# Q's first row block from exact codes in a PSUM bank of its own, and Q's cosine product on GpSimd

## The reference

```python
def _dequant(codes, scales):
    w = codes.astype(jnp.float32) - 8.0
    return w * jnp.repeat(scales, GS, axis=0)
...
q = hidden_states @ _dequant(q_codes, q_scales)
k = hidden_states @ _dequant(k_codes, k_scales)
v = hidden_states @ _dequant(v_codes, v_scales)
...
q = _rope(q)
k = _rope(k)
...
scores = jnp.einsum('bhqd,bhkd->bhqk', q, k) * scale + mask[None, None]
attn = jax.nn.softmax(scores, axis=-1)
out = jnp.einsum('bhqk,bhkd->bhqd', attn, v)
...
return out @ _dequant(o_codes, o_scales)
```

## Time and profile before

| | before |
|---|---|
| median of 3 runs | 1103.8 us (1103.57 to 1104.54) |
| span of the profiled execution | 1104.9 us, 18938 instructions |
| mean granted PE clock | 0.992 |
| PE busy | 96% |
| DVE busy | 85% |
| ACT busy | 63% |
| POOL busy | 62% |

### The profile page before, as it was taken

One profiled execution on the slowest core, in us unless ns is written; L12 is line 12 of the kernel. 1 busy time (PEld: TensorE's weight loads), 2 busy tenths in 40 slices (PEclk: granted clock), 3 DMA queues, 4 the chain that ended last, 5 costly groups with the idle time before them and its releaser, 6 DMA issues.

```text
span 1104.9 us, 18938 instructions
## 1 busy us (share of the span) xinstructions
PE 1056.7 (96%) x5448; PEld 513.8 (47%) x5448; DVE 934.1 (85%) x1755; ACT 690.9 (63%) x1502; POOL 689.6 (62%) x770
## 2 busy tenths in 40 slices
PE   3898999899999999999999999999999999989998
PEld 2443444444544444444444444544544544444443
DVE  7977897799888888888888889999999998888873
ACT  4455665766777777777777776666666666463320
POOL 2457546877767766776777677777878777332200
PEclk9999999999999999999999999999999999999999
DMA  9344231767678667657766765777777675432453
GB/s 350 123 135 132 67 101 44 150 149 170 142 155 160 145 147 159 159 134 154 163 148 141 159 160 130 148 155 162 151 150 171 142 128 119 108 117 53 101 103 79
DMA packets 301204, 153.65 MB, mean 139 GB/s; under 512 B 249264, under 2 KB 261808, under 8 KB 301136
## 3 DMA queue, kind: packets, MB, share of 16 engines
q1 hardware_dynamic: 293360, 139.46, 55.3%
q10 hardware_dynamic: 7776, 13.37, 4.4%
HBM read 89.07 MB, written 4.19 MB: 84 GB/s over the span
## 4 chain that ended last, share of the span: by engine, by line
PE 78%; DVE 8%; ACT 5%; POOL 3%; issue 3%; ACTq 1%; DMA 1%; SPq 1%; DVEq 0%; POOLq 0%
PE side_ps L699 10%; PE side_ps L856 9%; PE side_ps L701 9%; PE side_ps L700 9%; PE proj_ps L876 8%; PE out_ps L876 8%; PE proj_ps L1027 4%; PE score_ps L839 3%; PE score_ps L841 2%; PE score_ps L840 2%; PE proj_ps L1032 2%; PE score_ps L998 2%; PE out_ps L719 2%; PE score_ps L719 2%; PE proj_ps L699 2%
## 5 line engine op out<-in xcount | busy, mean ns | idle before, releaser
L1534 POOL TENSOR_TENSOR w_b<-prob,w_b 128x896 f16<-128x896 f32 (+2 forms) x192 | 188.9, 998 | 30.6 <-ACT w_b L1222 30.0
L699 PE MATMUL side_ps<-hT,w_a 128*128 128x512 f16 x504 | 191.1, 379 | 1.5 <-DVE rot L1895 1.5
L701 PE MATMUL side_ps<-hT,w_a 128*128 128x512 f16 x504 | 191.0, 379 | 0.0
L700 PE MATMUL side_ps<-hT,w_a 128*128 128x512 f16 x504 | 191.0, 379 | 0.0
L1990 DVE SCALAR_TENSOR_TENSOR x_acc<-proj_ps,o_now,x_acc 128x1024 f32<-128x1024 f32 x120 | 153.6, 1280 | 37.8 <-PE proj_ps L876 37.8
L1527 POOL TENSOR_SCALAR prob<-prob,row_inv 128x512 f32<-128x512 f32 (+3 forms) x256 | 170.7, 681 | 22.6 <-DVE row_inv L2063 16.9
L1195 ACT ACTIVATE prob<-score_ps,neg_max 128x512 f32<-128x512 f32 (+3 forms) x256 | 132.9, 521 | 47.4 <-DVE neg_max L1966 38.6
L1541 POOL TENSOR_TENSOR q_sb<-rot,q_sb 128x512 f16<-128x512 f32 x64 | 75.0, 1172 | 139.8 <-ACT q_sb L1187 139.8
L1990 DVE SCALAR_TENSOR_TENSOR x_acc<-out_ps,o_now,x_acc 128x1024 f32<-128x1024 f32 x120 | 152.7, 1272 | 0.0
L876 PE MATMUL proj_ps<-work,w_b 128*128 128x512 f16 x496 | 127.3, 379 | 1.9 <-DVE x_acc L1990 1.1
L876 PE MATMUL out_ps<-work,w_b 128*128 128x512 f16 x496 | 127.3, 379 | 1.3 <-DVE x_acc L1990 1.2
(11 more groups left out here) (238 smaller groups left out, 2102.5 us busy)
## 6 DMA issues: line engine op xcount, KB each, us to landing
stage_c<-in_codes_dram SPq DMA_DIRECT2D x80, 256.0 KB, 2.9
stage_o<-in_codes_dram SPq DMA_DIRECT2D x64, 256.0 KB, 3.9
stage_s<-in_scales_dram SPq DMA_DIRECT2D x64, 256.0 KB, 3.8
ctx_raw<-in_ctx_dram ACTq DMA_DIRECT2D x32, 256.0 KB, 3.2
work<-w_b SPq DMA_TRANSPOSE x261, 3.0
x_acc<-in_x_dram SPq DMA_DIRECT2D x8, 512.0 KB, 8.5
k_sb<-in_codes_dram SPq DMA_DIRECT2D x16, 256.0 KB, 6.4
v_sb<-in_scales_dram SPq DMA_DIRECT2D x16, 256.0 KB, 7.3
```

The costliest lines, as they stand in the source:

```text
L699: pe.matmul(o, stat(0), mov(0), start=first, stop=False)
L700: pe.matmul(o, stat(0), mov(1), start=False, stop=False)
L701: return pe.matmul(o, stat(1), mov(0), start=False, stop=last)
L1534: ins = pool.tensor_tensor(prob16[:, 1, to:to + w], prob[:, at:at + w], prob16[:, 0, to:to + w], ALU.subtract)
```

## The change

The first row block of Q's weights (row block 0 of 8) is no longer scaled ahead of the product. Its codes less 8 are whole numbers that float16 holds exactly, so there is no lower part: `q_exact` takes two products for it (codes by upper and by lower part of the hidden states) in place of three, into `pv_ps`, the bank of `weigh`. The scale, one for each feature and so for each partition here, is applied by ACT when it copies that bank to `rot` (`q_base`). `q_part` adds up row blocks 1 to 7 in `q_ps` as before, and DVE adds both (`q_join`) into `rot`. From there swap, cosine and sum read `rot`; the cosine product, in place, is POOL's (`q_turn`), and `sine` moves with it to the head of POOL's next slot. `q_sum` moves behind O add 3. Q's of slots 0 to 3 are made as before (`by_parts`). The scales for `q_base` ride with O's in `o_table` and `o_now`, one column more; they are loaded once (`q_scale_rows`) and scaled by DVE in the prologue. `k_scale` moves into a free part of `prob`.

```diff
+            def q_exact(g, i):
+                h = i // B
+                p = g * SLOTS + i
+                pe.wait_ge(piece_done, g * SLOTS + (2 * h + 2))
+                pe.wait_ge(ao_ready, p - 3)
+                for l in range(2):
+                    mm = pe.matmul(pv_ps, w_a[:, 0, h % RING * KB * P:(h % RING * KB + 1) * P],
+                                   hT[:, l, 0, i % B * S:(i % B + 1) * S], start=l == 0, stop=l == 1)
+                mm.then_inc(q_exact_done, 1)
...
                     else:
-                        pe.wait_ge(q_summed, p)
+                        pe.wait_ge(q_joined, p - FIRST_PIECES)
...
+                if not (known(p) and (p == 0 or p >= N_SLOTS - FIRST_PIECES + 1)):
+                    pe.wait_ge(q_based, p)
...
-                if has_ahead:
+                parts = by_parts(p + Q_AHEAD)
+                if has_ahead and parts:
+                    q_exact(*ahead)
+                elif has_ahead:
                     q_part(*ahead, range(0, 1))
...
+                if exact:
+                    act.activation(w[:, 0, col:col + exact], stage_c[:, r, 0:exact], ACT.Copy, bias=-CODE_ZERO)
+                act.activation(w[:, 0, col + exact:col + PIECE], stage_s[:, r, exact:PIECE], ACT.Copy, scale=up)\
                     .then_inc(piece_hi, 1)
...
-                swap(q_bank(p), q_swapped)
+                if by_parts(p):
+                    act.wait_ge(q_joined, p - FIRST_PIECES + 1)
+                swap(rot if by_parts(p) else q_bank(p), q_swapped)
+            def q_base(g, i):
+                p = g * SLOTS + i
+                act.wait_ge(q_exact_done, p - FIRST_PIECES + 1)
+                act.wait_ge(q_ready, p)
...
+                act.activation(rot[:, :], pv_ps, ACT.Copy, scale=o_now[:, (i // B + 1) % 2, CB:CB + 1])\
+                    .then_inc(q_based, 1)
...
                 if has_piece:
                     q_cut(p, i)
+                if has_ahead and by_parts(p + Q_AHEAD):
+                    q_base(*((g, i + Q_AHEAD) if i < SLOTS - Q_AHEAD else (g + 1, i + Q_AHEAD - SLOTS)))
...
+            def q_turn(p):
+                pool.wait_ge(q_swapped, p + 1)
+                pool.tensor_tensor(rot[:, :], rot[:, :], cos_t[:, :], ALU.mult).then_inc(q_cosed, 1)
...
                         pool.wait_ge(ctx_free, q + 1)
+                    if not (known(p) and p >= N_SLOTS - 1) and by_parts(p + 1):
+                        sine(q_swapped, p + 1, q_sined)
+                        q_turn(p + 1)
...
                     prob_rest(p, 0)
-                    if not (known(p) and p >= N_SLOTS - Q_AHEAD):
+                    if not by_parts(p + Q_AHEAD):
                         sine(q_swapped, p + Q_AHEAD, q_sined)
                     prob_rest(p, 1)
...
-                dve.tensor_tensor(rot[:, :], q_bank(p), swapped[:, :], ALU.add).then_inc(q_summed, 1)
+                dve.tensor_tensor(rot[:, :], rot[:, :] if by_parts(p) else q_bank(p), swapped[:, :], ALU.add)\
+                    .then_inc(q_summed, 1)
+            def q_join(p):
+                dve.wait_ge(q_done, p + 1)
+                dve.wait_ge(q_based, p - FIRST_PIECES + 1)
+                dve.tensor_tensor(rot[:, :], q_bank(p), rot[:, :], ALU.add).then_inc(q_joined, 1)
...
-                if has_next:
+                if has_next and not by_parts(p + 1):
                     q_sum(p + 1)
                 if not (i or known(p)):
-                    maxima(p, i, 0)
+                    dve.wait_ge(q_ready, p + 1)
                 if has_o and not (known(p) and p == O_LAG):
                     o_add(p - 1, (i - 1) % SLOTS, 3)
+                if not (i or known(p)):
+                    maxima(p, i, 0)
+                if has_next and by_parts(p + 1):
+                    q_sum(p + 1)
                 maxima(p, i, 1)
...
                 if has_o:
                     o_add(p, i, 1)
                 if known(p) and wf_early(p) is not None:
                     wf_difference(wf_early(p))
+                if has_ahead and by_parts(p + Q_AHEAD):
+                    q_join(p + Q_AHEAD)
                 if has_o:
                     o_add(p, i, 2)
...
-                if has_ahead:
+                if has_ahead and not by_parts(p + Q_AHEAD):
                     q_cos(p + Q_AHEAD)
```

## The result

| | before | changed |
|---|---|---|
| median | 1104.2 us (1103.57 to 1105.71, 4 runs) | 1222.1 us (1220.46 to 1222.34, 4 runs) |
| ratio | | 1.1058 (95% interval 1.1046 to 1.1071) |
| span of the profiled execution | 1104.9 us | 1218.7 us |
| mean granted PE clock | 0.992 | 0.982 |

What follows compares the result with a forecast made beforehand. A closed loop through DVE, ACT and POOL, not PE, was to bound the changed kernel: 34 (context) + 46 (dense-weight) + 9 (group 0) + 1 (prologue) = 90 us on 1104.9, median 1194 us, range 1160 to 1230.

Steps and rivals of the forecast that it cites:

- the loop: Closed slot-to-slot chain through DVE, ACT and POOL, without PE, longer than the old period; chance 0.78, 1194 us.
- the 1.8 us stop ahead of `q_sum`: On DVE after O add 3: the moved `q_sum` waits 1.8 us for POOL's cosine, everything queued behind it waits too.
- Context slots: Groups 1 to 4, 32 slots: loop of 13.22 us against 12.15, 1.07 more each, 34 us.
- Dense-weight slots: Slots from 40 on: loop of 14.05 us against 11.98, 2.07 more in 22 slots, 46 us.
- this collision: POOL and DVE slowing each other in the new order: bounded at 0.3 us per slot, 18 us.
- Group 0: Slots 3 to 7, of the dense-weight kind (slot 7 without POOL's weight add): about 9 us more.
- The cosine: POOL's cosine product in the loop: 1.27 us by the trace, against 1.38 us and 1200 us total by the skill's rule.
- `q_base`, counted at nothing: New PSUM eviction on ACT, 0.60 us by L1231, covered by ACT's wait for POOL; 36 us without that cover.
- Nothing of PE's 13 us is left.: 60 saved PE products of 0.22 us, 13 us at most, gain nothing since PE idles 1.5 to 2.3 us a slot.
- Had the loop been open: Rival, loop does not close: PE's saved products count for 6 to 13 us, 1091 to 1098 us; chance 0.05.
- The join counted as no gain and no loss on DVE: DVE loses the cosine product and gets `q_join` instead, both 128x512 from PSUM: nothing either way.
- PE's clock: Rival: idle time in each slot also lowers PE's clock, 50 us more, about 1244 us; chance 0.07.

Runs made afterwards that it cites:

- e5: Changed kernel with one extra small POOL product per slot (0.40 us) ahead of the sine, inside the loop: 1243.2 us, ratio 1.1244.
- e6: Changed kernel with the same extra POOL product of 0.40 us placed behind the cosine, beside the loop: 1226.0 us, ratio 1.1092.
- e1: Changed kernel with sine and cosine of Q(p+2) put back between POOL's two probability rests: 1135.0 us, ratio 1.0277.
- e2: Changed kernel with the cosine product back on DVE, sine still at the head of POOL's slot: 1155.6 us, ratio 1.0456.
- e8: Changed kernel with the weight difference and `q_join` moved ahead of O add 1 on DVE: 1157.4 us, ratio 1.0474.
- e9: Changed kernel with only the dense weights' difference moved ahead of O add 1, join left behind both: 1209.5 us, ratio 1.0950.
- e10: e7 with a third product in the exact block again (the second repeated): 1113.8 us, ratio 1.0082.
- e7: Changed kernel with the moves of e1 and e8 together: 1110.4 us, ratio 1.0046.
- e4: Changed kernel with `q_join` ahead of the weight difference on DVE in dense-weight slots: 1193.7 us, ratio 1.0806.
- e12: e7 with the join behind O add 1 again in the context slots only: 1112.8 us, ratio 1.0071.
- e3: Changed kernel with the pieces' scaling and lower part over all 512 columns again in even slots: 1227.8 us, ratio 1.1113.

## Why the prediction was right, and where it was off

The forecast was 1194 us, 90 more than before; it came out at 1222.1, 118 more, in the upper part of the range of 1160 to 1230.

**What bounds the kernel, and the loop.** The order of the links, the 1.8 us stop ahead of `q_sum` (1.69 measured) and that PE has no part held. e5 against e6 shows that time counts inside the loop and little beside it (21 against 4 us), and e1, e2 and e8 each take back what they take out of it, up to the next chain. What I had missed is that there are two loops with the join in common. It made no difference to the sum, which went by the longer; it would have made one to advice: the obvious cure (e1) leaves 30 us, by size more than half of it the long difference.

**Context slots.** The sum gave 13.22 us a slot, 34 us; 13.26 and 35.7 measured. It is not luck by terms that cancel: DVE's part from `q_sum` to the join was taken as 6.36 us and is 6.35, and no other link is off by more than 0.07.

**Dense-weight slots: the term that was mis-sized.** 14.05 us were predicted, 14.87 measured, 63.5 us in place of 46. The step taken was "777.78 to 783.80 (maxima 1 to the end of the weight difference) 6.02", with the difference at the earlier trace rows's 0.47 us. In ten of the 22 slots it takes 1.92, which is by size some 14.7 of the 17.5 us; e9, which takes it away, gets 0.43 a slot back. I had bounded this collision at 0.3 us a slot by the longest L1522 and L1764 and had looked at no instruction between them. The kernel before held it once already, in the maximum of the difference's own line, from the source view of L1913:

```profile
L1913 DVE SCALAR_TENSOR_TENSOR w_b<-w_b,wf_mean x31: 467/470/1709, 191.4 to 948.8; 128x256 f32<-128x256 f32 x31
```

That one began at 675.30, 0.45 us behind the begin of rest 0. The short slots, 14.23, are 0.18 us over the sum; 0.13 of that is `q_sum`, 0.82 us beside POOL's weight clip where the context slots have 0.69. Slots 60 and 61 are 0.70 under it, since they convert no piece.

**Group 0.** 9 us predicted, 15.3 measured. Two of its differences take 1.92 us, which is 2.9 of the 6.3 us more. The rest wasn't separated.

**The cosine.** 1.27 us by the earlier trace rows; its own row in the changed kernel, with those of `q_base` and `q_sum`:

```profile
L1591 POOL TENSOR_TENSOR rot<-rot,cos_t x60: 1254/1265/1276, 219.7 to 1044.4; 128x512 f32<-128x512 f32 x60
```

```profile
L1227 ACT ACTIVATE rot<-side_ps,o_now x60: 667/670/687, 211.6 to 1036.0; 128x512 f32<-128x512 f32 x60
```

```profile
L1953 DVE TENSOR_TENSOR rot<-rot,swapped x60: 691/693/827, 221.0 to 1045.8; 128x512 f32<-128x512 f32 x60
```

The row came closer than the rule of the Trainium skill ("GPSIMD Engine Reference", section Engine selection: about twice VectorE's time): 1.265 against 0.69 us is 1.8 times.

**`q_base`, counted at nothing.** 0.67 us, not the 0.60 of L1231; it stood under ACT's wait, as said. In context slots, where the split behind it waits for nobody, it is part of what delays ACT; the loop, which enters ACT at the swap, doesn't see it.

**"Nothing of PE's 13 us is left."** PE is idle for 13% of the changed kernel's span and its chain is not PE's; no run puts the product back there. Had the loop been open I gave 6 to 13 us for it; e10 measures 3.4.

**The join counted as no gain and no loss on DVE** was right in DVE's work (934.1 and 945.9 us busy, of which the twelve long differences alone add some 17), wrong as a way of seeing it: unlike the cosine that it replaces, ACT's swap waits for it.

**PE's clock.** The rival had a chance of 0.07. It came true in small: the view by windows of the changed kernel in dense-weight and in context slots,

```profile
700.00:800.00 100.00, 85.45 (x430) 40.21 (x428) 78.72 (x146) 59.50 (x143) 69.47 (x81) 0.97 0.55 126
...
500.00:600.00 100.00, 89.62 (x479) 44.02 (x478) 76.23 (x145) 71.62 (x161) 73.72 (x84) 1.00 0.61 137
```

and one place of it in PE's timeline:

```profile
850.64 1.86 PE L905 MATMUL proj_ps<-work,w_b 128*128 128x512 f16 x4 [2.73 <-DVE work L2079]
```

Four products take 1.86 us after 2.73 us of idle time, at a granted clock of 0.50 (1.2 GHz) from 850.6 to 852.5 us; four such took 1.03 in e7 at a clock of 1.00. The same idle time, 2.72 or 2.73 us, stands ahead of these products in all ten long slots: behind four of them they took 1.64 to 1.87 us, behind one 1.15, behind five 1.02. e4, e8 and e9, in which the 1.92 us is off the loop or gone, have a mean clock of 0.99. The Trainium skill ("TensorE: Matmul & The Clock Gate", section HAM oscillation) names waits between bursts of products as what brings the clock down. The trace agrees in that the slow products stand behind such a wait, and adds that not every equal wait has it. What it cost wasn't separated; `weigh` and the exponents aren't on the loop.

## What to carry to other kernels

A step moved to another engine is to be costed by the closed loop from one slot to the next through all in-order queues, not by the engines' idle time; list every loop that goes through the new wait, since opening the longest leaves the next. If an edit changes when a GpSimd operation begins, look which VectorE instructions then begin just behind it, and put those ahead of it; the maximum in the source view of such an instruction may show the collision before the edit. What a saved product is worth is read only where TensorE's work sets the period: here 3.4 of 13 us at best.

## What the runs showed of the hardware

A VectorE instruction of 0.47 us, with two SBUF inputs, took 1.92 us when it began 0.24 us after GpSimd's probability rest of 1.89 us (two SBUF inputs), and 1.79 us when it began 0.38 us after it; both ended 0.27 to 0.28 us after that instruction's end. In e4 it took 1.89 and 1.32 us when begun 0.28 and 0.84 us after it, again ending 0.28 us after its end. Begun 0.32 us ahead of it, it took 0.47. So it isn't slowed in proportion but held to the other's end, and who begins first decides. A copy of nine columns from SBUF to SBUF was held to the end of GpSimd's cosine (0.95 in place of 0.39 us) and ended 0.03 us after it; in e1's dense-weight slots it began 0.04 us ahead of the cosine and took 0.16. `q_sum`, 512 columns, ended 0.54 us after the extra operation of e6. The piece behind the other's end grows with the columns: 0.03, 0.28 and 0.54 us for 9, 256 and 512. O adds (L2063, from PSUM with one SBUF input stream, 1.27 us) kept their time beside the same rest. The Trainium skill ("GPSIMD Engine Reference", section Specifications) says that the two engines share SBUF interfaces and that there is contention for VectorE instructions with two SBUF inputs or in a two-port mode. The traces agree for the instructions with two SBUF inputs, and add how hard they are hit; in which mode the copy runs no view shows.

ACT stood still for 1.5 to 1.7 us at each turn of the hardware loop in e1, e2, e7 and e12, 0.7 to 0.8 in the changed kernel and e3, and no more than in any slot, 0.16, in before. In e8 it was 1.0 to 1.2. ACT's instructions are the same in all these but before, which has fewer; the cause stays open.
